# Earlier slot copy, later softmax sums and earlier layer-norm statistics in a fused attention and mixture-of-experts layer

## What is computed

```python
xn = _layernorm(x)
# deformable attention: 8 heads, 4 points each
off = (xn @ W_off + b_off).reshape(8, 1024, 8, 4, 2)
w   = softmax((xn @ W_attn + b_attn).reshape(8, 1024, 8, 4), axis=-1)
idx = clip(wrap(off[..., 0].astype(int32)), 0, 127)
g   = take_along_axis(xn[:, 0, :], idx)          # values of the batch's first token
s   = sum(g * w, axis=(heads, points))           # one number per token
att = broadcast(s, 128) @ W_out + b_out
# feed-forward: 2 shared experts, and the 2 best of 8 routed experts
ffn(x, w1, w2, w3) = silu(x @ w1.T) * (x @ w3.T) @ w2.T
rw, sel = top_k(xn @ router_w.T + expert_bias, 2); rw = softmax(rw)
out = x + att + sum_shared ffn(xn) + sum_selected rw * ffn_e(xn)
```

## Time and profile before

| | |
|---|---|
| median of three runs | 430.51 us (430.02 to 431.07) |
| profiled execution, its own time | 431.98 us |
| its span, first to last instruction | 430.1 us |
| mean granted TensorE clock | 0.958 of full speed |
| PE busy | 374.9 us (87%) |
| DVE busy | 333.2 us (77%) |
| ACT busy | 189.1 us (44%) |
| POOL busy | 190.4 us (44%) |

### The profile page before, as it was taken

The page is one execution under the profiler, slowest core; times in us unless marked ns, Lnnn a source line. Parts: engine busy times, 40 slices in busy tenths (PEclk is TensorE's granted clock), DMA queues, the critical chain, the costliest instruction groups (busy, mean ns, idle before and its releaser), DMA issues.

```text
span 430.1 us, 12600 instructions
## 1 busy us (share of the span) xinstructions
PE 374.9 (87%) x4349; PEld 323.8 (75%) x4349; DVE 333.2 (77%) x930; ACT 189.1 (44%) x447; POOL 190.4 (44%) x153
## 2 busy tenths in 40 slices
PE   0155584989999999999999999999999999999990
PEld 0155543667677777777778999999999999999990
DVE  5877889966956789999998798897666676666660
ACT  3678337584422256666667444432222222222220
POOL 0434400402877775333310000000588888888883
PEclk9986698799999999999999999999999999999995
DMA  8954610000111969977788335556456666554442
GB/s 301 278 110 99 138 40 1 0 2 13 36 52 59 164 110 167 173 156 156 156 127 130 40 101 160 122 127 150 72 61 78 64 65 77 62 64 39 40 39 18
DMA packets 98870, 41.35 MB, mean 96 GB/s; under 512 B 73600, under 2 KB 92416, under 8 KB 98816
## 3 DMA queue, kind: packets, MB, share of 16 engines
q1 hardware_dynamic: 87120, 31.82, 36.1%
q0 software_dynamic: 11264, 8.69, 15.2%
q10 hardware_dynamic: 432, 0.11, 0.1%
HBM read 10.94 MB, written 12.88 MB: 55 GB/s over the span
## 4 chain that ended last, share of the span: by engine, by line
PE 76%; DVE 11%; ACT 6%; DMA 2%; issue 1%; POOL 1%; POOLq 0%; DVEq 0%; ACTq 0%
PE pY L823 17%; PE pY L656 11%; PE pAB L796 8%; PE pAB L797 8%; PE pAB L795 8%; PE pAB L641 5%; PE pAB L643 5%; PE pAB L642 5%; PE pV L668 3%; ACT units L861 3%; DVE hbuf L1182 2%; PE pV L619 1%; ACT wsp L921 1%; DMA xT<-hot 1%; PE pV L582 1%
## 5 line engine op out<-in xcount | busy, mean ns | idle before, releaser
L1054 POOL DMA_INDIRECT out_dram<-xT,rows x64 | 99.1, 1548 | 105.4 <-DMA out_dram<-base 86.2
L1042 POOL DMA_INDIRECT sorted_rows<-rows,slot x64 | 67.8, 1059 | 70.7 <-issue 35.7
L998 ACT ACTIVATE units<-pAB 128x512 f32<-128x512 f32 x78 | 46.5, 596 | 119.6 <-PE pAB L797 112.8
L796 PE MATMUL pAB<-rows,wsp 128*128 128x128 f16 x512 | 89.0, 219 | 0.0
L795 PE MATMUL pAB<-rows,wsp 128*128 128x128 f16 x512 | 89.0, 219 | 0.0
L797 PE MATMUL pAB<-rows,wsp 128*128 128x128 f16 x512 | 89.0, 219 | 0.0
L823 PE MATMUL pY<-wsp,hbuf 128*128 (+1 forms) x620 | 86.4, 282 | 0.3 <-issue 0.3
L1459 DVE SCALAR_TENSOR_TENSOR hbuf<-pAB,units 128x512 f32<-128x512 f32 x78 | 53.6, 687 | 32.0 <-PE pAB L797 30.7
L823 PEld LDWEIGHTS pY<-wsp,hbuf 128*128 128x128 f32 x620 | 75.6, 192 | 0.8 <-issue 0.5
L939 ACT ACTIVATE units<-pAB 128x512 f32<-128x512 f32 x64 | 38.1, 596 | 82.3 <-PE pAB L643 82.2
L656 PE MATMUL pY<-wsp,hbuf 128*128 128x128 f32 x512 | 70.4, 281 | 0.0
(11 more groups left out here) (167 smaller groups left out, 609.2 us busy)
## 6 DMA issues: line engine op xcount, KB each, us to landing
base<-in_x SPq DMA_DIRECT2D x8, 512.0 KB, 7.3
out_dram<-base SPq DMA_DIRECT2D x16, 256.0 KB, 2.4
wraw<-in_wall SPq DMA_DIRECT2D x10, 256.0 KB, 2.7
rows<-hot SPq DMA_DIRECT2D x8, 256.0 KB, 2.7
proj<-sorted_rows SPq DMA_DIRECT2D x27, 68.5 KB, 2.0
wsp<-in_wall SPq DMA_DIRECT2D x10, 128.0 KB, 3.9
sorted_rows<-rows,slot POOLq DMA_INDIRECT x64, 2.4
out_dram<-xT,rows POOLq DMA_INDIRECT x64, 3.6
```

Source lines behind the costliest of these rows:

```text
L796: pe.matmul(o, hi, x(1), start=False, stop=False)
L1042: pool.indirect_dma_start(sorted_rows, bass.IndirectOffsetOnAxis(ap=slot[:, t:t + 1].bitcast(U32), axis=0), rows[:, t, :], None, bounds_ch ...
L1054: pool.indirect_dma_start(out_rows, bass.IndirectOffsetOnAxis(ap=meta[:, t, DEST - CW:DEST - CW + 1].bitcast(U32), axis=0), yt[:, t], None ...
```

## The change

In the prologue, the statistics of blocks 10 to 15 move to earlier steps of DVE's loop (blocks 10 and 11 by one step, 12 and 13 by one, 14 by one, 15 by two), `variances(3)` from step 9 to 8, `scales(3)` from step 10 to 9, and ACT's `root(3)` from step 9 to 8.

In the units, the call of `shared_unit()` behind the clip and the one behind the sums of the exponentials are taken out of their places, and the slots' copy moves ahead of these sums. No unit is dropped: those two are then done in the loop that fills up to unit 24. PE's `PLACE_UNIT` goes from 11 to 10 and its `TABLE_UNIT` from 14 to 12; ACT's `ABS_UNIT`, `WHOLE_UNIT` and `SIGN_UNIT` go from 13, 14, 15 to 11, 12, 13. The wait for ACT's sign moves to the piece that uses it.

```diff
--- before.py
+++ after.py
@@ -80,7 +80,7 @@
 ROUND = 8
 PARTS = [(0, 2), (2, 5), (5, 10), (10, 16)]
 PART_OF = [k for k, (lo, hi) in enumerate(PARTS) for _ in range(lo, hi)]
-ROOT_AT = {1: 1, 2: 4, 3: 9}
+ROOT_AT = {1: 1, 2: 4, 3: 8}
 PROJ_LAG = 4
 SENT = NB // 2
 LOW_BY_DVE = 4
@@ -92,8 +92,8 @@
 TURNS = 4
 
 ROWS_UNIT = 4
-GAP_UNIT, SEG_UNIT, TAB_UNIT, PLACE_UNIT, TABLE_UNIT = 3, 6, 8, 11, 14
-OFFSET_UNIT, LOGIT_UNIT, ABS_UNIT, WHOLE_UNIT, SIGN_UNIT = 7, 10, 13, 14, 15
+GAP_UNIT, SEG_UNIT, TAB_UNIT, PLACE_UNIT, TABLE_UNIT = 3, 6, 8, 10, 12
+OFFSET_UNIT, LOGIT_UNIT, ABS_UNIT, WHOLE_UNIT, SIGN_UNIT = 7, 10, 11, 12, 13
 SPREAD_UNIT = UNITS - 4
 REG_LOAD = 4
 PACE_FROM, PACE = 9, 50
@@ -1124,13 +1124,13 @@
                     scales(1)
                 if i == 5:
                     scales(2)
-                if i == 10:
+                if i == 9:
                     scales(3)
-                for later in {1: (5,), 2: (6, 7), 3: (8, 9), 5: (10,), 6: (11,), 7: (12, 13), 8: (14,), 9: (15,)}.get(i, ()):
+                for later in {1: (5,), 2: (6, 7), 3: (8, 9), 4: (10,), 5: (11,), 6: (12, 13), 7: (14, 15)}.get(i, ()):
                     block_statistics(later)
                 if i == 4:
                     variances(2)
-                if i == 9:
+                if i == 8:
                     variances(3)
                 if i == NB - 1:
                     dve.wait_ge(csum_done, 1)
@@ -1275,7 +1275,6 @@
             for r in range(4):
                 dve.wait_ge(row_in[r], 16 * (SENT // 4))
             v.tensor_scalar(offsets, offsets, 127.5, -128.0, ALU.min, ALU.max).then_inc(clipped, 1)
-            shared_unit()
 
             assert unit[0] > OFFSET_UNIT + 1
             dve.wait_ge(offset_added, 2)
@@ -1295,15 +1294,13 @@
             v.memset(seg[:, 2, 1:2], 0.0).then_inc(tsel_ready, 1)
             shared_unit()
 
+            assert unit[0] > PLACE_UNIT
+            dve.wait_ge(place_done, 1)
+            v.tensor_copy(slot[:], pV[:, 1, 256:256 + NT]).then_inc(slot_ready, 1)
             assert unit[0] >= LOGIT_UNIT
             dve.wait_ge(logit_exp, 1)
             then(v.tensor_tensor(halves4, weight4[:, :, :, 0:2], weight4[:, :, :, 2:4], ALU.add))
             then(v.tensor_tensor(wmax[:, 1], halves4[:, :, :, 0], halves4[:, :, :, 1], ALU.add))
-            shared_unit()
-
-            assert unit[0] > PLACE_UNIT
-            dve.wait_ge(place_done, 1)
-            v.tensor_copy(slot[:], pV[:, 1, 256:256 + NT]).then_inc(slot_ready, 1)
             by_two = wmax[:, 1].rearrange("p t (k h) -> p t k h", k=2)
             then(v.tensor_tensor(sum_pairs, by_two[:, :, 0], by_two[:, :, 1], ALU.mult))
             two_pairs = sum_pairs.rearrange("p t (k h) -> p t k h", k=2)
@@ -1329,16 +1326,17 @@
             ins.then_inc(table_ready, 1)
             shared_unit()
 
-            assert unit[0] >= SIGN_UNIT
+            assert unit[0] >= WHOLE_UNIT
             dve.wait_ge(clipped, 1)
+            dve.wait_ge(size_ready, 2)
+            dve.wait_ge(cw_ready, 1)
+
+            then(v.scalar_tensor_tensor(fl[0], whole, 0.0, size, ALU.add, ALU.is_gt))
+            shared_unit()
+            then(v.tensor_tensor(fl[1], whole, fl[0], ALU.subtract))
+            shared_unit()
+
             dve.wait_ge(size_ready, 3)
-            dve.wait_ge(cw_ready, 1)
-
-            then(v.scalar_tensor_tensor(fl[0], whole, 0.0, size, ALU.add, ALU.is_gt))
-            shared_unit()
-            then(v.tensor_tensor(fl[1], whole, fl[0], ALU.subtract))
-            shared_unit()
-
             then(v.tensor_tensor(idx3, fl[1], signs, ALU.mult))
             shared_unit()
             then(v.tensor_scalar(ilo, idx3, LO16 - 1, None, ALU.bitwise_and))
```

More of the change, by code:

```diff
@@ L1330, in _ @@
             shared_unit()
-            assert unit[0] >= SIGN_UNIT
+            assert unit[0] >= WHOLE_UNIT
             dve.wait_ge(clipped, 1)
-            dve.wait_ge(size_ready, 3)
+            dve.wait_ge(size_ready, 2)
             dve.wait_ge(cw_ready, 1)
@@ L1340, in _ @@
             shared_unit()
+            dve.wait_ge(size_ready, 3)
             then(v.tensor_tensor(idx3, fl[1], signs, ALU.mult))
```

## The result

The changed kernel took 435.97 us (median of 5 runs: 433.9, 435.97, 435.73, 436.16, 436.37), the kernel before 430.31 beside it on the same chip: a ratio of 1.0118, 95% interval 1.0095 to 1.0141, or 5.7 us slower. The forecast was 432.6 with a range of 429.9 to 433.5: slower was right, the size was not. The profiled execution is the quickest of the five (433.9; span 432.0, mean clock 0.976; the other four had mean clocks of 0.948 to 0.952), so that part of the loss is missing from its profile.

A forecast was written before the change was run, and what follows sets the result against it. PE, gapless from 114.78 us on, was taken to bound the kernel, so the moment it becomes gapless counts. Statistics -1.1, order +1.6 and clock +1.6 made +2.1 on the median 430.51: 432.6 us, range 429.9 to 433.5 (own range 431.7 to 433.4).

The forecast's parts named there:

- Part 1, the statistics: Prologue: statistics moved earlier remove ACT's 1.36 us wait and start the routing sooner; gain 1.1 us, bounds 0.7 to 1.36.
- Part 2, units and slots: Shared units up to 19: the new order makes PE idle longer, mainly ahead of line 619; loss 1.6 us, bounds 1.2 to 2.0.
- the clock stays up: Rival at line 619: TensorE's clock doesn't fall behind the idle time; +0.5 us, 431.0 us; chance 0.26.
- Part 3, the clock: Line 619: the clock falls behind 2.9 us of idle PE; 3.2 us of work at half speed costs 1.6 us.
- half of 4.36: Upper bound of the clock's cost at line 619, 2.2 us, from PE's busy time during a prologue stretch at 1.2 GHz.
- worked gaplessly from 51.95 to the rise: Prologue row: 3.65 us of gapless PE work before the clock rose, used in taking 3.2 us at half speed for line 619.
- all of it is on the path: Line 619: the whole 1.6 us lost to the lower clock was claimed to lengthen the kernel.
- The prologue's gain is multiplied: Rival: earlier clock rise before unit 7's products starts the placing 1.4 us sooner; -0.9 us, 429.6 us; chance 0.16.
- The gain is lost: Rival in the prologue: something other than DVE's casts sets the routing's start, the statistics give nothing; +3.2, 433.7 us; chance 0.08.

The follow-up runs named there:

- the filled gap: The changed kernel with 12 unused 512-column products in PE's idle time ahead of line 619: 431.12 us, ratio 1.0016 to the kernel before, on the calm chip.
- the units alone: Kernel before with only the units and slots moved, statistics as before: 446.98 us (ratio 0.9935) and 446.3 us (0.9941), on chips with stops.
- the second experiments: A later group on another chip with stops; its repeat of the unaltered change took 446.54 us, ratio 0.9931 to the kernel before (449.3 us).

## Why the prediction was wrong

**Part 1, the statistics (-1.1): agrees, but was not timed alone in calm conditions.** ACT's wait is gone and the meeting with POOL costs 0.87 us (1.08 - 0.21). The mean start of the routing is 1.1 us sooner (55.82 - 54.69, above). The ratios of this part alone make -1.3, -0.5 and -1.6 us of some 449, all on chips with stops, and the second of them can't be told from none. The Trainium skill ("SBUF — State Buffer", section Who interferes with whom), by which this meeting was certain, agrees with the rows at 30.73 and 30.83.

**Part 2, units and slots (+1.6): held.** Idle time ahead of line 619 was 2.72 us (forecast 2.9), and DVE's wait 4.01 us when the clock stays (forecast 4.0). Of the later waits of PE (forecast 0.27, 1.27 and 0.20) the profile with the filled gap has 0.23, 1.16 and 0.25, the outer two worked out from start to start. In it the first products of unit 19 come 115.96 - 53.71 = 62.25 us behind the first reduction, before 60.58: +1.67. With the clock kept up, parts 1 and 2 together measured 431.12 - 430.64 = +0.5 us: -1.1 + 1.6. That kernel is the first rival, "the clock stays up", made to happen.

**Part 3, the clock (+1.6, at most 2.2): the step that failed.** That the clock would fall was forecast and came true in all seven profiles in which line 619 stood unchanged behind idle time of 1.8 to 2.7 us. Its price was too small by a factor of three: 4.4 to 5.3 us from median to median (446.54 - 441.27, 446.54 - 442.14, 436.1 - 431.12). The upper bound, "half of 4.36", was taken from a stretch of projections, and the argument that PE "worked gaplessly from 51.95 to the rise", 3.65 us, assumed that the clock would be back as soon here. It was not: it stood at 0.50 through 7.24 us of line 619's gapless work and was back 2.7 us behind it. In the rows of after, line 619 from start to start takes 97.74 - 87.92 = 9.82 instead of 6.27 us, +3.55; then come 2.76 us of work at half clock, +1.4; in sum 4.95.

That "all of it is on the path" did not hold either. Unit 19 comes 65.21 - 62.25 = 3.0 us later in this profile than in the one with the filled gap, since PE, being later, no longer waits 1.16 us for unit 12, and line 619 began 0.6 us sooner behind the reduction. Over all profiles the difference is 3.5 us (mean 65.77 in the four of the change, 62.24 in the three with the filled gap), and 4.0 in the ordinary execution of the second experiments (66.26). The rest, up to the 4.4 to 5.3 of the medians, is in large part that three of the four profiled executions of the change were 0.9 to 2.1 us quicker than their median. So 4.95 is near the measured price by chance. With 5.0 in the place of 1.6 the sum is +5.5, and the first timing gave +5.66; this closes because the 5.0 and the +0.5 were both measured on the calm chip.

The forecast's own range, 431.7 to 433.4, was also drawn too narrow by its own terms: with the clock's upper bound of 2.2 it would have reached 434.0. The measured 435.97 lies above that as well.

**The other rivals.** "The prologue's gain is multiplied": the placing started 85.75 - 53.71 = 32.0 us behind the first reduction, 0.8 less than the forecast's 32.8 (89.2 - 56.39), so that about half of this rival's 1.4 us was there. It is not the gain's doing, since the units alone, with the old statistics, have 32.6 and 31.8. The rival's other condition, that the clock doesn't fall at line 619, failed, and no execution of the change on a calm chip came near 429.6. "The gain is lost" would have left the filled gap at +1.6 us, where +0.5 was measured.

**The sign.** The change is 5.5 us slower on the two calm chips and 3 us faster on the two chips with stops where it was timed. No row of the kernel before in its profile could have told this, since that profile has no stop. Forecast and first timing are of the calm kind, and that the forecast was put to the test in calm conditions was luck.

## What to carry to other kernels

When work is moved so that PE idles ahead of a long line, price the clock for that whole line and the products right behind it, as it was down here, and not for a few microseconds; a bound that comes from a row of another kind of work is no bound. Then look which later waits catch a part of the delay. A gap that can't be closed can be filled: twelve useless products cost nothing here and gave about 5 us back. And before a wait on which an engine will idle anyway, look for what is queued behind it that doesn't need it: the two sums, moved ahead of it, gave 1.5 us on the calm chip.

## What was not expected of the hardware

- Behind an idle time of 2.7 to 2.8 us, and of 1.82 us in one kernel, TensorE fell to 1.2 GHz and stayed there through 7.2 us (first timing), 10.0 us (the units alone, below) and, with 192-column products between, 12.8 us of work without a gap, and was back about 2 to 5 us behind line 619 in all of them. Behind the same 2.83 us it did not fall in the one profile with 512-column products in line 619. Windows of the units alone, on the chip where they took 446.3 us:

```profile
86.38:89.10 2.72, 0.01 (x1) 0.03 (x1) 2.17 (x2) 2.70 (x7) 0.00 (x0) 1.00 0.00 0
...
90.50:100.50 10.00, 10.00 (x49) 10.00 (x49) 0.96 (x4) 1.95 (x2) 0.00 (x0) 0.50 0.00 0
100.50:103.50 3.00, 3.00 (x13) 2.11 (x13) 2.76 (x5) 0.00 (x0) 1.36 (x1) 0.50 0.00 0
104.00:108.00 4.00, 4.00 (x28) 2.94 (x27) 3.90 (x8) 3.65 (x4) 3.02 (x4) 1.00 0.16 53
```

- The same kernel before took 430.3 to 430.6 us on two chips and 448.1 to 449.8 on four. On those four, the profiles of the other kernels show stops in which three engines stand still together, mostly with nothing recorded that they wait for. Fewer scatters in the stretch took 8 us of the 18 away.
